# Third attention's keys computed during the expert tiles, and parts of the product-key and normalization work moved to GpSimd, in a new hand-written order

## The chip, the cores and the metric

One core of one Trainium2 chip runs the whole program in a single launch. The metric is the device time of that core in microseconds (us), as the median of several executions; lower is better. The engines are TensorE (PE: matmuls and transposes; its weight loads are listed apart as PEld), VectorE (DVE), ScalarE (ACT), GpSimd (POOL, which also issues some DMAs) and SyncE (SP, which here only issues DMAs).

## The reference

The input x is 2048 rows of 256 numbers. Eight sublayers follow each other, each of the form x = x + f(layernorm(x)). Besides x, the attentions read a context ctx of 16 x 128 rows of 128 numbers.

```
x = x + attention 1        (32 heads of 8, axial rotation of q and k)
x = x + product-key FFN    (4 heads: top 8 of 128 twice, top 8 of the 64 sums, 2048 experts)
x = x + attention 2        (16 query heads, 8 key/value heads of 128)
x = x + router, top 2 of 7 experts of width 256, and one shared expert
x = x + attention 3        (16 heads of 16, q and k layer-normalised per head)
x = x + ternary FFN        (width 682)
x = x + attention 4        (16 heads of 128, q and k RMS-normalised)
x = x + MXFP8 FFN          (width 1024)
```

The third attention treats the last 16 of each 128 context rows apart, with weights of their own:

```
y_dca, y_main = y[:, -16:], y[:, :-16]
k_dca, v_dca = split(y_dca @ Wkv_dca + bkv_dca);  k_dca = ln(k_dca, kn_dca_w, kn_dca_b)
q = ln(x @ Wq + bq, qn_w, qn_b)
k = ln(y_main @ Wk + bk, kn_w, kn_b);  v = y_main @ Wv + bv
out = (attn(q, k, v) + attn(q, k_dca, v_dca)) @ Wo + bo
```

`ln` works on each head's 16 numbers. Note that k and v of this attention depend on ctx and on weights alone, and not on x.

In the product-key FFN each row finds, for each of 4 heads, 8 pairs of keys. The kernel turns them into weights of experts by masks that are compared and multiplied, so that PE can do the gather as matmuls.

## The kernel before, in words

x stays in on-chip memory as 16 blocks of 128 rows. The work is cut into sublayers `s` (0 attention 1, 1 product-key FFN, 2 attention 2, 3 router, 8 expert tiles, 9 shared expert, 4 attention 3, 5 ternary FFN, 6 attention 4, 7 MXFP8 FFN), each of these into named steps per block `b` and part `c`, and `STEPS` says for each step on which engines it has instructions. Blocks of neighbouring sublayers run interleaved: a block needs only itself from the sublayer before, except where a table `ROOM` asks that an earlier sublayer is finished, because both use the same on-chip memory.

What sets the order is a text written by hand for each engine: in `ORDER` one letter stands for one step, and the n-th occurrence of a letter is the n-th part of that step. The engines run their queues in this order and wait for each other by counted semaphores (`wait_ge`). `BANKS` says which of the eight PSUM banks a step's result takes; `room` makes PE wait until the engine named in `TAKEN` has emptied the bank's previous content.

The steps that the change and the prediction touch, with the lines of the kernel before:

- Attention 3 (`small_heads` with s = 4): `qk` multiplies the block by Wq (L955, L956) and the context block by Wk (L960), and adds the last 16 context rows by Wkv_dca (L961), into one bank of 512 columns; `na` (DVE adds the bias, L1843; ACT squares), `nb` (DVE sums the squares per head, L1849; POOL adds epsilon and takes the power -1/2 of 128 x 32 numbers, L2526), `nc` (DVE multiplies, L1855), `tqk` (PE transposes q in four and k in four pieces, L990; ACT scales them into qT and kT), `vp` (values, L973, and those of the last 16 rows, L974), `mx` (score matmuls L1008, of which DVE takes the row maxima, and the same line again for the scores proper in `st`), and `tb`, `oT`, `out` for the result. POOL copies the last 16 context rows of every block into a tile of its own (L2503).
- Product-key FFN (`peer`): `ix` picks the indices of the 8 best pairs (DVE: compare L1946, multiply L1950, reduce L1952, each twice on 256 columns), `ae` makes a one-hot mask of 512 columns, `am` multiplies it by three parts of the weight (L2001, three times on 512 columns, four times per block), and `g` is the matmul on it.
- `lnA` and `lnB` normalise a block: statistics on DVE, the power on POOL, and the subtraction and multiplication on DVE (L1759).
- Router: `tab` (with a cast at L2133) makes the table of where rows go, `sc` scatters them by POOL's DMA into 38 tiles in DRAM (L2582), SP loads each tile (six tiles are in flight), the tiles run `tT`, `up`, `ga`, `dn` (L1200 to L1225), and POOL stores each (L2598). `cw` centres the third attention's weights on DVE, `init` fills its tiles on POOL (L2471 to L2492).

The step that reads a tile's matrices waits for the tile's load; POOL's store waits for ACT's result.

Of the kernel before, what the change touches and what calls it, by code (L numbers as in the profile page):

```python
# [28 lines left out]
RP, RQ, RV = 4, 3, 2  # L29

# [29 lines left out]
}  # L60
# [19 lines left out]
        "qwoppnooppwqplowompnlowpmoorpqnplopmonpoorlpooqmpnlooompxponpqppoolopxqprpomppnoooqlpopmoonolppmqppooolppxonqpopmoop"  # L80
        "pnxqppoxoppowrqppooosppxotosspqpttsssptpsttqtxsstusuxtuurvvvvsstutsrusvvtsytzuussttvvuttCusssutvvyuzvvrtussrututCsvv"
        "AuuAvvtBssytzuuBsvvsttvuurvssCuuttvrsvytvuttuzvsstsAsCuuvvyuvvBtsrttzsssAuutBvvuytzsuvvytCtuusszttyvuvvCussztuAvtruv"
        "vuAssCsyuzvvBttrtssAtutBsCusyvrtzuuBvvvsAsttystutCuzvvAuuBvvtBsssCtrtuutssCvyutzuvAvvtBussutytzuuCvvvrvAssAtytzuussB"
        "uttBvvAuBvvAuuCvyIBvzJuuCvvIIAJBKCJIIKyKzJJIIKKCJJADBKKEEFEEFFGGEFFHHEGEFFHEGGEFHHEGGEFFHEHFGEGFEHHEGGFFHHEGGEFFEHHF"
        "GEGFHEFGFHHEGGEFHHEFGGEFHHEGEGFFHHFEGGFEHHFEGGFHHEGEFEGFHHEFGGEFHHEGGFHEHEGGFFHHEGGFHHFGGHHIIJJIIIKKJJIIKKLJMJLKIIML"
        "JJLMJKKKNOPNKMPQONRSSSSTTPQONLRMUPSVQSSSTORTQLSNUSMSSRLTTOMUPSSVLLNVQPSSMTROTSSNSSQPOMTURTQLSSVNSSRTLTOPUNVSPUSQSSMO"
        "MRLTTQVSSMTSSRUTLLONVMPZZUSSSSNTOQPMLTLRVNSSZZQSSPNOTMTURQVSSPSSNTZORTMUSSSSPOQTWTWRQUSSVNSSRTONPSWXTSSSPOQXVQRTTUXW"
        "SSXWYWXWXSSRTWXXYYUXXVSSSSTTUYWXWXVTXXYVXUXYWXVXUYVXXWYYWXXXYWXXXXWYYXXX61W60Y60XXY6YY6262616120-1--1321312032234112"
        "34551410532314251322431455231403541253-241-52433524114-5530372121424123355438145531723124245432850124755432348811952"
        "+3453145510298137238142523134+1452455398871+4312432254559113+08435212487317504221455933+1130221435288421133245454355"  # L90
        "0988374+113422542591543+53288274215103432415915132831+84035231124245745523435198811732+41345504232159784+53318241228"
        "54859247373+4553898348784+45545598879+88+9+9+"),
    "V": (
        "ayahy((byabaabcabacbbacbaabdaeeceedeeceebaeeeeeeceedeebbeeffeecegedaeebefe(feeceedgeeeefceefebedeegaaeeffceeaeedbbgb"
# [2626 lines left out]
```

## Time and profile before

| what | value |
| --- | --- |
| median of 3 timed runs | 1972.67 us |
| lowest and highest of them | 1969.64 and 1978.3 us |
| the profiled execution | 1967.78 us, of this its span 1966.0 us |
| granted clock of TensorE, mean | 0.994 |
| PE busy | 1886.6 us (96%) |
| DVE busy | 1641.7 us (84%) |
| ACT busy | 1259.4 us (64%) |
| POOL busy | 791.2 us (40%) |

The span runs from the first to the last instruction. PE is busy for nearly all of it, so the share of the other engines says little by itself; what counts is in which stretch PE stands and for whom. A granted clock of 1.00 is PE's upper level of 2.4 GHz; 0.5 would be the lower of 1.2 GHz. The stages follow each other roughly so: attention 1 to 210 us, product keys to 550, attention 2 with the router to 938, tiles to 1070, attention 3 to 1270, ternary FFN to 1350, attention 4 and the MXFP8 FFN to the end.

### The profile page before, as it was taken

What the parts mean: (1) busy time and instruction counts of PE and PEld (TensorE: products, weight loads), DVE (VectorE), ACT (ScalarE), POOL (GpSimd) and SP (SyncE); (2) the same over time, 40 slices, a digit from 0 to 9 for tenths busy, and PEclk for the clock granted to TensorE, in tenths of its full rate; (3) what the DMA queues carried; (4) which work ended last, traced back from release to release, by engine and by line L of the source; (5) the groups of instructions that cost most, each with busy time, mean ns of one, the idle gap of its engine ahead of it and who ended that gap; (6) DMA issues with size and microseconds to landing.
All of it is one profiled execution on the core that took longest, in us unless ns stands there. A gap on an engine that the chain in (4) does not pass through costs nothing. (4 is left out here: it accounts for less than half of the span.)

```text
span 1966.0 us, 44931 instructions
## 1 busy us (share of the span) xinstructions
PE 1886.6 (96%) x15558; PEld 1502.2 (76%) x15558; DVE 1641.7 (84%) x4453; ACT 1259.4 (64%) x3210; POOL 791.2 (40%) x1160
## 2 busy tenths in 40 slices
PE   5999999999999999999799899999999999999999
PEld 3777899999988888888698777897565666566656
DVE  6888999999879987886755689886888998988897
ACT  3878988788865445554465566865676655656652
POOL 6443020000011223222213987513877666666640
PEclk9999999999999999999899999999999999999999
DMA  9500300000034434434222011016776455555540
GB/s 327 185 2 3 110 27 2 2 2 2 2 120 128 150 119 134 157 118 133 80 85 68 28 28 55 2 62 209 245 227 218 151 168 159 185 174 169 183 145 28
DMA packets 223642, 215.82 MB, mean 110 GB/s; under 512 B 25934, under 2 KB 198120, under 8 KB 222392
## 3 DMA queue, kind: packets, MB, share of 16 engines
q1 hardware_dynamic: 197176, 129.29, 21.7%
q0 software_dynamic: 26240, 83.65, 11.9%
q8 instruction: 125, 2.05, 0.4%
q14 instruction: 101, 0.83, 0.1%
HBM read 115.85 MB, written 96.99 MB: 108 GB/s over the span
## 5 line engine op out<-in xcount | busy, mean ns | idle before, releaser
L2462 POOL TENSOR_SCALAR sm<-sm 128x1 f32<-128x1 f32 x128 | 34.7, 271 | 503.8 <-DVE sm L1749 502.9
L1516 ACT ACTIVATE areaB<-i128h,workB 128x128 f16<-128x128 f16 x512 | 156.4, 393 | 0.5
L1677 ACT ACTIVATE workA<-pb,workA 128x128 f32<-128x128 f32 x256 | 113.8, 458 | 28.6 <-DVE workA L2343 26.5
L1090 PE MATMUL pb<-areaB 128*128 128x128 f32 x1024 | 123.2, 277 | 0.5 <-ACT workB L1506 0.5
L1134 PEld LDWEIGHTS pb<-xT,areaA 128*128 128x128 f32 x1024 | 119.1, 192 | 5.8 <-issue 5.1
L1134 PE MATMUL pb<-xT,areaA 128*128 128x128 f32 x1024 | 121.0, 275 | 0.0
L1090 PEld LDWEIGHTS pb<-areaB 128*128 128x128 f32 x1024 | 117.8, 192 | 2.0 <-ACT workB L1506 0.9
L1324 PE MATMUL pb<-areaA,workA 128*128 128x256 f32 x512 | 118.9, 380 | 0.1
L1468 ACT ACTIVATE areaA<-pb 128x512 f32<-128x512 f32 x192 | 105.2, 604 | 21.6 <-PE pb L1008 20.8
L2534 POOL DMA_DIRECT2D turn<-workA x64 | 36.9, 577 | 202.4 <-DVE workA L2046 194.2
L1157 PE MATMUL pb<-areaA,workA 128*128 128x256 f32 x512 | 117.2, 380 | 0.0
L1324 PEld LDWEIGHTS pb<-areaA,workA 128*128 128x128 f32 x512 | 96.0, 190 | 26.9 <-issue 14.8
L1106 PE MATMUL pb<-areaB,workB 128*128 128x256 f32 x512 | 113.9, 380 | 0.3 <-DVE workB L2010 0.3
L1543 ACT ACTIVATE workA<-workA 128x128 f32<-128x128 f32 x256 | 99.4, 392 | 19.1 <-DVE workA L2033 19.1
L1157 PEld LDWEIGHTS pb<-areaA,workA 128*128 128x128 f32 x512 | 95.3, 190 | 15.3 <-issue 3.5
L1106 PEld LDWEIGHTS pb<-areaB,workB 128*128 128x128 f32 x512 | 96.1, 190 | 13.5 <-DVE workB L2010 0.7
L1870 DVE TENSOR_REDUCE workA<-pb 128x4 f16<-128x512 f32 x128 | 83.0, 690 | 15.8 <-PE pb L1008 15.3
L2526 POOL TENSOR_TENSOR areaA<-areaA,neghalf 128x32 f32<-128x32 f32 x16 | 87.4, 5463 | 1.3
L1008 PE MATMUL pb<-workA 32*128 32x128 f16 (+2 forms) x2048 | 78.5, 251 | 8.4 <-DVE workA L1873 3.2
L2464 POOL TENSOR_TENSOR sm<-sm,neghalf 128x1 f32<-128x1 f32 x128 | 81.5, 637 | 10.7
L1310 PEld LDWEIGHTS pb<-workA 128*128 128x128 f32 x512 | 65.1, 191 | 26.7 <-issue 18.0
L1008 PEld LDWEIGHTS pb<-workA 32*128 32x128 f16 (+2 forms) x2048 | 57.5, 140 | 33.6 <-issue 28.5
(425 smaller groups left out, 5638.7 us busy)
## 6 DMA issues: line engine op xcount, KB each, us to landing
turn<-workA POOLq DMA_DIRECT2D x64, 256.0 KB, 2.5
workA<-turn SPq DMA_DIRECT2D x256, 64.0 KB, 2.1
turn3q<-workA POOLq DMA_DIRECT2D x64, 256.0 KB, 2.9
turn3k<-areaA POOLq DMA_DIRECT2D x64, 256.0 KB, 2.8
workB<-turn3q SPq DMA_DIRECT2D x256, 64.0 KB, 2.3
workA<-turn3k SPq DMA_DIRECT2D x256, 64.0 KB, 2.1
turn3p<-areaA POOLq DMA_DIRECT2D x64, 256.0 KB, 2.7
rows_in<-areaB SPq DMA_DIRECT2D x7, 2048.0 KB, 16.1
```

The costliest lines, as they stand in the source:

```text
L1008: m = eng.matmul(p[k][:, j * 128:(j + 1) * 128], one, two, start=True, stop=True)
L1090: m = eng.matmul(p[:, e * 128:(e + 1) * 128], w.ed[:, k, (4 * c + e) * 128:(4 * c + e + 1) * 128], xT[:, k, :], start=(k == 0), stop=(k == 1))
L1106: m = eng.matmul(p[:, 0:256], G[:, e, :], w.eu[:, e, :], start=(e == 0), stop=(e == 15))
L1134: m = eng.matmul(p[:, h * 128:(h + 1) * 128], w.wq[:, 4 * c + h, k], xT[:, k, :], start=(k == 0), stop=(k == 1))
L1157: m = eng.matmul(p[:, 0:256], u.OT[i][:, h], w.wo[:, 4 * c + h], start=(c == 0 and h == 0), stop=(c == 3 and h == 3))
L1324: m = eng.matmul(p[:, 0:256], u.OT[i][:, h], w.wo[:, 4 * c + h], start=(c == 0 and h == 0), stop=(c == 3 and h == 3))
L1468: eng.activation(u.P[n % RP], bank(s, tag, b, at)[:, :], ACT.Exp, scale=1.0 / math.sqrt(hd)).then_inc(freed(s, tag, b, at)[0], 1)
L1516: m = eng.activation(u.far[:, g], i128h[:, :], ACT.Square, bias=u.at[b % 2][:, 8 * c + g:8 * c + g + 1])
L1543: m = eng.activation(u.P[i][:, h], u.P[i][:, h], ACT.Exp, accum_out=u.den[i][:, h:h + 1], bias=u.nm[i][:, h:h + 1])
L1677: m = eng.activation(u.P[i][:, h], p[:, h * 128:(h + 1) * 128], ACT.Exp, accum_out=u.den[i][:, h:h + 1], bias=u.nb[i][:, h:h + 1], scale=u ...
L1870: eng.tensor_reduce(o[:, :, 24:25], p, AX.X, ALU.max, negate=True).then_inc(freed(s, tag, b, at)[0], 1)
L2526: eng.tensor_tensor(va, va, neghalf[:, 0:32], ALU.pow).then_inc(S["l2_rs"], 1)
```

## The change

It has three parts and a new order text for all engines.

1. **Keys early.** A new sublayer 10 of 18 blocks (`KEYS = NB + 2`) computes the third attention's keys while the expert tiles run. Its blocks 0 and 1 hold the last 16 context rows of eight context blocks each, so that one matmul of 512 columns gives keys and values of all of them; blocks 2 to 17 are the keys of the 16 context blocks. Each goes through bias, square, sum, power (now 128 x 16), multiplication, four transposes and scaling, and is written to DRAM (`keys4`, and `vals4` for the values). The third attention reads its keys and the 16 value rows back by SP (steps `kl`, `vl`). Its own `qk`, `na`, `nb`, `nc` handle q alone, on 256 columns, `vp` is one matmul and one copy, and the matmul on the difference of weights and POOL's copies are gone. The shared expert's `dn` uses bank 6 alone, and the keys use bank 7 for both steps.
2. **Product keys.** One compare of 512 columns instead of two of 256, the multiplication on POOL, one reduction; the third of the three masks of `am` is multiplied on POOL; the one-hot tile has two buffers.
3. **Normalization.** The subtraction and multiplication of `lnB` in attention 1 and in the product-key FFN move from DVE to POOL (`centred`).

```diff
-    1: (("lnA", 1, "VG"), ("lnB", 1, "V"), ("xT", 1, "TA"), ("q", 1, "TA"), ("sim", 1, "TA"), ("g", 4, "TA"),
-        ("tk", 1, "V"), ("tx", 1, "V"), ("pk", 1, "V"), ("ix", 1, "V"), ("tr", 1, "V"), ("bh", 4, "A"), ("ae", 4, "V"),
-        ("am", 4, "VT"), ("gm", 4, "V"), ("out", 1, "TV")),
+    1: (("lnA", 1, "VG"), ("lnB", 1, "G"), ("xT", 1, "TA"), ("q", 1, "TA"), ("sim", 1, "TA"), ("g", 4, "TA"),
+        ("tk", 1, "V"), ("tx", 1, "V"), ("pk", 1, "V"), ("ix", 1, "VG"), ("tr", 1, "V"), ("bh", 4, "A"), ("ae", 4, "V"),
+        ("am", 4, "VGT"), ("gm", 4, "V"), ("out", 1, "TV")),
...
+    10: (("k", 1, "T"), ("ka", 1, "AV"), ("kv", 1, "VG"), ("kc", 1, "V"), ("kt", 1, "TA"), ("ks", 1, "S")),
...
-        "eeabaababaacadbdcdbadfdZagdbdgehhhghdcigdfhhhhdgbigdhjhhhgdkcigafdhhehhgdbigdahhhjhdkcgfadghihhdbhdgihgehhdgchjgdfkh"
+        "Zaababbaacedbdcdbedaaafdgdbdghhahgdhecigdfhhhhdgbigdhjhhhgdkcgifdhhhhagdbigdahhhjhdkcgidfahhgdbhhgdeigdhehgcjhhghfdh"
...
-    (9, "dn"): lambda b, c: (("dn", 6 + b % 2),),
+    (9, "dn"): lambda b, c: (("dn", 6),),
...
+    (10, "k"): lambda b, c: (("k", 7),),
+    (10, "kt"): lambda b, c: (("kt", 7),),
...
+            def early_keys(step, b):
+
+                if step == "k":
...
+                    if b < 2:
+                        t.wait_ge(S["l2_init"], 1)
+                        m = eng.matmul(p[:, :], u10.last[b], w4.wd, start=True, stop=True)
+                    else:
+                        m = eng.matmul(p[:, 0:256], ctxT[:, (b - 2) * 128:(b - 1) * 128], w4.wk, start=True, stop=True)
+                    m.then_inc(full(10, "k", b)[0], 1)
+                else:
+                    t.wait_ge(S["l2_y"], b + 1)
+                    kp4 = u4.qp[b] if b < 2 else u10.kp[b % 2]
+                    p = room(10, "kt", b)
+                    for j in range(4):
+                        m = eng.transpose(p[:, j * 128:(j + 1) * 128], kp4[:, j * 128:(j + 1) * 128], ident)
...
+            def early_keys(step, b):
+                va = u10.va[b % 2]
+                g.wait_ge(S["l2_var"], b + 1)
+                eng.tensor_scalar(va, va, 1.0 / 16, 1e-6, ALU.mult, ALU.add).then_inc(*g.mark())
+                g.settle()
+                eng.tensor_tensor(va, va, neghalf[:, 0:16], ALU.pow).then_inc(S["l2_rs"], 1)
+
+            def peer(step, b, c):
+                u = u1
+                if step == "ix":
+                    g.wait_ge(S["v_next"], b + 1)
+                    e4 = u.eq.rearrange("p (h k j) -> p h k j", h=8, k=8)
+                    eng.tensor_tensor(e4, e4, bc(u.i8f.rearrange("p (h j) -> p h j", h=8), 2, [128, 8, 8, 8]),
+                                      ALU.mult).then_inc(S["g_pre"], 1)
+                elif step == "am":
...
+                    eng.tensor_tensor(u.Am[c % 2][:, 2], u.Ae[c % 2],
+                                      bc(ah[:, 3, 8 * c:8 * c + 8].rearrange("p (h g) -> p h g", g=2), 2, [128, 4, 64, 2]),
+                                      ALU.mult).then_inc(S["g_mul"], 1)
```

How the order text moves instructions is seen in the built programs, at three places.

POOL, between the router's last scatters (`rows_in`) and the stores of the tiles (`rows_out`); `workA` is on-chip memory that attention 3 will use. Before:

```order
L2462 TENSOR_SCALAR sm<-sm 128x1
L2464 TENSOR_TENSOR sm<-sm,neghalf 128x1
L2582 DMA rows_in<-areaA,workB 15104x256 x4
L2471 MEMSET workA 128x1024 x2
L2474 MEMSET workA 128x128 x3
L2476 MEMSET workA 128x1024 x2
L2490 TENSOR_SCALAR workA<-cst 128x16 x2
L2492 TENSOR_SCALAR workA<-cst 128x16 x2
L2490 TENSOR_SCALAR workA<-cst 128x16 x2
L2492 TENSOR_SCALAR workA<-cst 128x16 x2
L2598 DMA rows_out<-areaA 128x256 x38
```

After:

```order
L2594 MEMSET workA 128x1024 x2
L2609 COPY workA<-ctxT 128x128 x2
L2613 TENSOR_SCALAR workA<-cst 128x16 x4
L2615 MEMSET workA 128x16
L2616 MEMSET workA 128x16
L2615 MEMSET workA 128x16
L2616 MEMSET workA 128x16
L2724 DMA rows_in<-areaA,workB 15104x256 x6
L2740 DMA rows_out<-areaA 128x256
L2649 TENSOR_SCALAR areaA<-areaA 128x16
L2651 TENSOR_TENSOR areaA<-areaA,neghalf 128x16
L2740 DMA rows_out<-areaA 128x256 x6
```

The fills now stand ahead of the last three scatters, and the keys' powers stand between the stores of the tiles.

PE, in the tiles. Before (L1200 and L1201 transpose a tile, L1208, L1217 and L1224 to L1225 are its three matmul layers):

```order
L1208 MATMUL pb<-areaA 128x128 x8
L1224 MATMUL pb<-areaA 128x256
L1225 MATMUL pb<-areaA 128x256
L1224 MATMUL pb<-areaA 128x256
L1225 MATMUL pb<-areaA 128x256
L1200 MATMUL pb<-cst,areaA 128x128
L1201 MATMUL pb<-cst,areaA 128x128
L1217 MATMUL pb<-areaA 128x128 x4
```

After (L1116 is a key's matmul, L1123 its four transposes):

```order
L1116 MATMUL pb<-areaA,ctxT 128x256
L1281 MATMUL pb<-areaA 128x128 x4
L1272 MATMUL pb<-areaA 128x128 x4
L1264 MATMUL pb<-cst,areaA 128x128
L1265 MATMUL pb<-cst,areaA 128x128
L1288 MATMUL pb<-areaA 128x256
L1289 MATMUL pb<-areaA 128x256
L1288 MATMUL pb<-areaA 128x256
L1289 MATMUL pb<-areaA 128x256
L1123 MATMUL pb<-cst,workA 128x128 x4
```

Between a key's matmul and the next transposes PE now has one tile's matmuls or somewhat more.

DVE, in the product-key FFN, where the indices of a block are picked. Before:

```order
L1940 CAST workB<-workB 128x64
L2001 TENSOR_TENSOR areaB<-workB 128x512 x3
L1946 TENSOR_TENSOR workB<-cst,workB 128x256
L1950 TENSOR_TENSOR workB<-workB 128x256
L1952 TENSOR_REDUCE workB<-workB 128x32
L1946 TENSOR_TENSOR workB<-cst,workB 128x256
L1950 TENSOR_TENSOR workB<-workB 128x256
L1952 TENSOR_REDUCE workB<-workB 128x32
L1954 SCALAR_TENSOR_TENSOR workB<-workB 128x32
```

After:

```order
L2048 TENSOR_SCALAR workB<-workB 128x32
L2050 CAST workB<-workB 128x64
L2052 TENSOR_TENSOR workB<-cst,workB 128x512
L2056 TENSOR_REDUCE workB<-workB 128x64
L2058 SCALAR_TENSOR_TENSOR workB<-workB 128x32
```

Two compares, two multiplications and two reductions have become one compare and one reduction, with POOL's multiplication between them.

## Rows read from the trace of the kernel before

**Rows 1.** The page's line of busy time, share of the span and instructions.

```profile
PE 1886.6 (96%) x15558; PEld 1502.2 (76%) x15558; DVE 1641.7 (84%) x4453; ACT 1259.4 (64%) x3210; POOL 791.2 (40%) x1160
```

**Rows 2.** Windows: length, then busy PE, PEld, DVE, ACT, POOL, clock, DMA share, GB/s.

```profile
50.00:210.00 160.00, 156.61 (x2630) 116.81 (x2632) 135.61 (x337) 129.87 (x241) 59.07 (x114) 1.00 0.17 57
210.00:550.00 340.00, 335.23 (x3673) 314.00 (x3664) 310.37 (x1332) 297.03 (x728) 24.83 (x48) 1.00 0.06 21
...
938.00:948.00 10.00, 0.50 (x3) 0.09 (x1) 9.48 (x22) 1.24 (x2) 5.98 (x14) 0.77 0.04 14
948.00:1070.00 122.00, 120.05 (x893) 112.89 (x894) 66.06 (x142) 71.57 (x200) 23.67 (x41) 0.98 0.26 83
1070.00:1270.00 200.00, 187.16 (x2175) 156.78 (x2173) 160.37 (x459) 128.52 (x268) 158.59 (x140) 0.98 0.11 33
```

**Rows 3.** Timeline of PE in attention 3: start, duration, line [idle before <-releaser].

```profile
1118.96 1.09 PE L990 MATMUL pb<-cst,workA 128*128 128x128 f32 x8 [0.36 <-DVE workA L1855]
1119.88 0.27 PE L934 MATMUL pb<-cst,xn 128*128 128x128 f32 x1
...
1121.70 1.17 PE L1008 MATMUL pb<-workA 18*128 18x128 f32 x32 [1.44 <-DVE workA L1873]
...
1123.77 0.59 PE L960 MATMUL pb<-areaA,ctxT 128*128 128x256 f32 x2
1124.20 0.59 PE L961 MATMUL pb<-areaA,workA 128*128 128x256 f32 x2
1124.63 0.27 PE L1052 MATMUL pb<-cst,areaA 128*128 128x128 f32 x1
```

**Rows 4.** Groups of DVE in attention 3, 1070 to 1270 us.

```profile
L1855 DVE TENSOR_TENSOR workA<-workA,areaA 128x512 f32<-128x512 f32 x16 | 11.8, 740 | 4.4 <-POOL areaA L2526 3.6 <-PE pb L1018 0.8
...
L1849 DVE TENSOR_REDUCE areaA<-areaA 128x32 f32<-128x512 f32 x16 | 10.8, 676 | 2.2 <-ACT areaA L1426 2.1
```

**Rows 5.** Groups of POOL: busy, mean ns of one, idle before.

```profile
L2526 POOL TENSOR_TENSOR areaA<-areaA,neghalf 128x32 f32<-128x32 f32 x16 | 87.4, 5463 | 1.3
...
L2568 POOL TENSOR_TENSOR workA<-workA,neghalf 128x4 f32<-128x4 f32 x64 | 71.3, 1113 | 5.3
```

**Rows 6.** Timeline of PE in attention 4, two matmuls of 512 columns.

```profile
1409.88 1.02 PE L1294 MATMUL pb<-areaA,xT 128*128 128x512 f32 x2
1410.74 1.02 PE L1295 MATMUL pb<-areaA,xT 128*128 128x512 f32 x2
```

**Rows 7.** Groups of DVE by shape in the product keys, 210 to 540 us.

```profile
L2001 DVE TENSOR_TENSOR areaB<-workB 128x512 bf16<-128x512 bf16 x93 | 33.8, 417 | 0.2
...
L1950 DVE TENSOR_TENSOR workB<-workB 128x256 f32<-128x256 f32 x30 | 12.7, 425 | 1.0
```

**Rows 8.** Windows of 4 us in attention 3, columns as in rows 2.

```profile
1107.00:1111.00 4.00, 2.11 (x40) 1.71 (x39) 3.09 (x10) 3.23 (x5) 3.83 (x3) 0.96 0.01 2
...
1199.00:1203.00 4.00, 2.61 (x39) 1.84 (x32) 2.87 (x12) 2.46 (x7) 4.00 (x1) 0.98 0.00 0
...
1111.00:1115.00 4.00, 3.51 (x35) 3.37 (x36) 0.00 (x0) 2.65 (x6) 3.51 (x3) 0.61 0.00 0
1203.00:1207.00 4.00, 4.00 (x16) 3.46 (x16) 3.97 (x6) 2.85 (x6) 2.28 (x3) 0.59 0.00 0
```

**Rows 9.** Attention 4: POOL's products (group, one), DVE's L1759 (one; group from 1450 us).

```profile
L2562 POOL TENSOR_TENSOR workA<-workA 128x512 f32<-128x512 f32 x64 | 67.3, 1053 | 35.9 <-DVE workA L2348 35.1
...
1502.88 1.03 POOL L2562 TENSOR_TENSOR workA<-workA 128x512 f32<-128x512 f32 x1
...
1502.99 1.06 DVE L1759 TENSOR_SCALAR areaB<-x,sm 128x256 f32<-128x256 f32 x1
...
L1759 DVE TENSOR_SCALAR areaB<-x,sm 128x256 f32<-128x256 f32 x14 | 7.1, 511 | 2.0 <-POOL sm L2464 2.0
```

**Rows 10.** Timeline of the gap ahead of the tiles, one DVE and one POOL row.

```profile
936.05 4.84 DVE L2133 CAST workB<-workB 128x8 uint32<-128x8 f32 x1
...
939.00 1.86 POOL L2476 MEMSET workA<- 128x1024 f32 x2
```

More of the change, by code:

```diff
@@ L80 @@
[L80 to L83, printed above, removed]
@@ L1451, in small_heads @@
                     src = bank(4, "v", b)[:, 0:256].rearrange("p (h e) -> p h e", e=16)
-                    for k in range(2):
-                        m = eng.activation(u.vt[b % RV][:, :, 17 * k:17 * k + 16], src, ACT.Copy, scale=side[k])
-                    m.then_inc(freed(4, "v", b)[0], 1)
+                    eng.activation(u.vt[b % RV][:, :, 0:16], src, ACT.Copy, scale=in_main).then_inc(freed(4, "v", b)[0], 1)
                 elif step == "vp":
@@ L1486, in small_heads @@
                         m.then_inc(freed(s, "oT", b)[0], 1)
+            def early_keys(step, b):
+                u = u10
+                if step == "ka":
+                    a.wait_ge(*freed(10, "k", b))
+                    if b >= 2:
+                        a.wait_ge(S["l2_var"], b - 1)
+                    eng.activation(u.sq[b % 2], u.y[b % 2].rearrange("p (h e) -> p h e", e=16),
+                                   ACT.Square).then_inc(S["l2_sq"], 1)
+                else:
+                    a.wait_ge(*loaded(4))
+                    a.wait_ge(*full(10, "kt", b))
+                    if b in (2, 3):
+                        a.wait_ge(S["k_d"], 160)
+                    elif b >= 4:
+                        a.wait_ge(S[f"hbm{b % 2}"], 16 * (b // 2))
+                    src, dst = bank(10, "kt", b)[:, :].rearrange("p (t n) -> p t n", n=128), u.kT[b % 2]
+                    if b < 2:
+                        m = eng.activation(dst, src, ACT.Identity, scale=w4.nwc[:, 2:3], bias=w4.nwc[:, 5:6])
+                    else:
+                        m = eng.activation(dst[:, :, 0:112], src[:, :, 0:112], ACT.Identity, scale=w4.nwc[:, 1:2], bias=w4.nwc[:, 4:5])
+                    m.then_inc(freed(10, "kt", b)[0], 1)
             def peer(step, b, c):
@@ L2472, in small_heads @@
                     if s == 4:
-                        for k in range(3):
-                            eng.memset(u.cd[k], 0.0)
+                        for k in range(2):
+                            eng.memset(u10.kp[k], 0.0)
                     for k in range(RV):
@@ L2487, in small_heads @@
                         ones = ones_sq[:, 0:16].unsqueeze(2)
+                        g.wait_ge(*ctx_here(0))
+                        g.wait_ge(*ctx_here(NB - 1))
+                        for k in range(2):
+                            eng.tensor_copy(u10.last[k].rearrange("p (b n) -> p b n", n=16),
+                                            ctxT[:, :].rearrange("p (b n) -> p b n", n=128)[:, 8 * k:8 * k + 8, 112:128])
                         for j in range(2):
@@ L2609, in gpsimd_program @@
                     normalize(s, b)
+                elif step == "lnB" and s == 1:
+                    centred(1, b)
                 elif s in (0, 4):
                     small_heads(s, step, b, c)
+                elif s == 10:
+                    early_keys(step, b)
                 elif step == "ws":
@@ L2617, in gpsimd_program @@
                     tiles(step, b, c)
+                elif s == 1:
+                    peer(step, b, c)
                 elif s == 2:
```

411 lines of the change are left out of this document (244 added, 167 removed), and 6 rows, old and new, of tables (STEPS, TAKEN).

## The prediction

> **What bounds the kernel now.** The line of busy time comes first [rows 1]: TensorE (PE) is busy 1886.6 of 1966.0 us, VectorE (DVE) 1641.7, GpSimd (POOL) 791.2. So a step is paid for where PE executes it, and everything else pays only through the 79 us in which PE stands. Next come the windows by stage [rows 2]: in each the reader compares PE's busy time with the length, and then looks at who else is nearly full. Attention 1 (50 to 210 us) leaves PE 3.4 us idle and the product keys (210 to 550) 4.8, with DVE at 310.37 of 340 there. Between router and expert tiles (938 to 948) nearly all of the 10 us is lost. The tiles (948 to 1070) run PE 120.05 of 122 while DVE, ACT and POOL have half or more of their time free. The third attention (1070 to 1270) has the largest loss that the change touches, 12.8 us, with POOL at 158.59 and DVE at 160.37 of 200. The timeline of PE in that stage [rows 3] names what it waits for there: the normalised heads (1.44 us before the score matmuls L1008, 0.36 us before the transposes L990, both released by DVE). The groups of DVE [rows 4] go one step back: of the 4.4 us that it stood before L1855, 3.6 ended with POOL's power L2526, which takes 5.46 us [rows 5].
>
> **Part 1, the matmuls.** Per block the third attention loses three 256-column calls (L960, L961, L974) and four of its eight L990 transposes. From start to start a call takes 0.43 us (1123.77, 1124.20, 1124.63) and the eight transposes 0.92 us (1118.96 to 1119.88) [rows 3], so 3 x 0.43 + 0.46 = 1.75 us leave per block, 28.0 us in 16. Into the tiles come 16 calls of 256 columns (6.9 us), two of 512 at 0.86 [rows 6] (1.7) and 18 x 4 transposes (18 x 0.46 = 8.3): 16.9 us. The tiles have no idle PE time to hide them in, so they are paid in full. Net: **-11.1 us**. This part is nearly certain, since it is the same work at the same price.
>
> **Part 2, what the third attention gets besides.** POOL's power goes from 128x32 to 128x16. No row shows 16 columns; 4 columns take 1.11 us and 32 take 5.46 [rows 5], which are the two ends. Between them 28 columns cost 4.35 us, 0.155 each, so I take 1.11 + 12 x 0.155 = 2.97 us. POOL then has 16 x 2.5 = 40 us less work in this stage and its link of the chain is 2.5 us shorter. Three DVE passes of 512 columns (0.74 and 0.68 us, the third put at 0.68 too, [rows 4]) become 256 wide, for which 0.42 is the row of a pass of that width [rows 7]: 16 x 0.84 = 13.4 us. But PE's work falls from 187.16 to 159.2 and the stage with it, to about 167 us, in which DVE still needs 160.37 - 13.4 = 147, 88% against 80% now. A shorter chain wins back idle time and a fuller DVE costs some: of 12.8 us I take **-5**, with 0 and -12 as ends. In addition two stretches of 4 us ran with a granted clock of 0.61 and 0.59 [rows 8], so mostly at the lower level of 1.2 GHz, and in the 4 us ahead of each PE had been busy for only 2.11 and 2.61 us, at a clock of 0.96 and 0.98. At 0.6 of the clock 4 us lose 1.6; if those waits go, **-3.2**; ends 0 and -3.2.
>
> **Part 3, the product keys and attention 1.** DVE gives away one of three expert masks four times per block (0.417 us each, 64 in all: 27 us) and the index product; two compares, two products and two reductions of 256 columns (the product's 0.425 taken for all six, 2.55 us) become one compare and one reduction of 512, 0.68 each by L1849: 1.19 x 16 = 19 us [rows 4, 7]. The row normalisation (L1759; I take 0.41, the length of a pass of 256 columns [rows 7], though its mean in the last stage is 0.511 [rows 9]) goes to POOL in both stages, 6.5 us each. That is 52 us of 310 in stage 1. PE is idle there for only 4.8 us in 340, and 3.4 in 160 in attention 1, so the relief can show only in these 8.2 us: I take **-3**, ends 0 and -8. The new double buffer of the one-hot removes a wait on the same engine and is in that sum.
>
> **Part 4, the gap ahead of the tiles.** A cast of eight columns on DVE took 4.84 us there, to 940.89, while POOL filled buffers until 940.86 [rows 10]; nothing in its size explains more than some tenths. In the new order the fills stand ahead of the last scatters, so this cast is freed: about -4.5. Against it, all weights of the third attention are centred before the router's last steps: passes of 256 columns at 0.42 over wq, wk, wd and three biases, some 16 passes or 7 us of DVE, which the router's chain may have to wait for, and the last three scatters are queued on POOL behind fills, copies and small constants (1.86 for the fills of 1024 columns, the rest put at twice that). I take **0**, ends -5 and +7.
>
> **Part 5, the keys in the tiles off PE.** Per key: DVE 3 x 0.42, ACT one square and one scaling (put at 1.1 together, twice the share of a DVE pass), POOL one power at 2.97 and a small pass ahead of it, put at 0.3. For 18 keys that is 23 us on DVE (66.06 of 122 busy), 20 on ACT (71.57) and 59 on POOL (23.67) [rows 2], in a stage that grows to about 139 us. All fit, so the work costs nothing as long as no one waits in order; that condition is the rival E. DMAs: ten small writes, 16 key writes and 32 reads on SP's queue, on which the tile loads stand six tiles ahead of their use (6 x 3.2 = 19 us), and the DMA engines are busy for 0.26 of the stage. Cost 0.
>
> **Sum.** -11.1 - 5 - 3.2 - 3 + 0 = -22.3. The profiled execution took 1967.78 us (span 1966.0), so 1945.5. The median of the three timed runs, 1972.67, lies 4.9 us higher, so I forecast **1950**.
>
> **What the skill says against it.** A POOL pass over SBUF can hold DVE up: L1759 on DVE ran 1.06 us beside a 1.03 us product of POOL on 512 columns [rows 9], which is 0.65 us more than 0.41, the price that I put on this pass. The group shows how seldom: 14 of these passes in the last stage average 0.511 [rows 9], 0.1 us more each. The Trainium skill's page GPSIMD Engine Reference, section 1 (Specifications), says that GpSimd shares its SBUF interfaces with VectorE and contends with instructions in a two-port mode or with two SBUF inputs, and its section 4.1 advises VectorE for elementwise products, as GpSimd is about 2x slower. The trace agrees on speed: 1.05 us for 512 columns on POOL against 0.68 on DVE (L1849) [rows 4, 9]. Read strictly, the rule makes this change a loss in the product keys, which is rival D.
>
> **The rivals.**
> - **A, the forecast** (gain of 12 to 32 us, 1941 to 1961). For it: PE full everywhere but in the places named. Chance 0.50.
> - **B, only the matmuls count**: -11.1 and the third attention now bound by DVE (147 of 167). 1972.7 - 11 = 1962. Against it: the wait of 3.6 us on the power. 0.18.
> - **C, more idle is won**: all of the 12.8 and 8.2 us, the clock and 5 of the gap: -11.1 - 12.8 - 3.2 - 8.2 - 5 = -40, 1932, or lower where the new order also closes idle time outside the touched stages. 0.10.
> - **D, POOL's products hold DVE in the product keys.** Five products per block, 80 in all, 1.05 us each. If each held a DVE pass as L1759 was held (1.06 - 0.41 = 0.65 us), DVE would lose 52 us, all that it was relieved of; with its queue in order the masks also come later by 1.05 - 0.42 us. PE would gain nothing there and lose some 10 us to waits: 1972.7 - 11.1 - 5 - 3.2 + 10 = 1963, and 1973 with 20. Against it: the mean of 0.511, and the power of 5.46 us with POOL busy for 79% of the third attention, in which DVE's L1849 keeps 0.68. 0.12.
> - **E, slower: the keys stall the tiles.** Bank 7 serves both a key's matmul and its transposes, and a key runs through DVE, ACT, DVE, POOL (3 us) and DVE, about 6 us, before PE may transpose; a tile passes each 122/38 = 3.2 us, and PE's new order has some one to three tiles of work between the two. POOL issues the power in one queue with the stores of the tiles, which wait for ACT, so a power may come a tile late. If each of 18 keys costs one tile's time: 58 us, about 2008. The forecast is lost at (1962.8 - 1950)/18 = 0.7 us per key, and the kernel is measurably slower from (1982.6 - 1950)/18 = 1.8 us per key. 0.10.
>
> **How the numbers follow.** 0.5%, 9.9 us, is about what a measurement of this kernel can tell from no change: faster means below 1962.8, slower above 1982.6. All of A and C and half of B are faster (0.50 + 0.10 + 0.09), with a little of D: 0.70. Same: half of B, most of D, the mild part of E: 0.19. Slower: 0.11. The range leaves out the strong cases of E and the far part of C: 1922 to 1972. The likeliest case's own range is 1941 to 1961.
>
> **What would show it.** Tile stage: about 17 us longer and PE still full; if PE waits for bank 7 or for L1123's input there, E. Third attention: about 33 us shorter, power near 3 us, no stretch at half clock; if it is 28 shorter with PE waiting for DVE, B. Product keys: PE's idle time down from 4.8; if DVE's busy time stays near 310 in spite of the 52 us removed, with casts and scalar passes at over 1 us, D. The gap of 10 us: the 4.84 us cast gone and PE's first tile no later than before; if the centring passes stand between the router's last steps, part 4 was wrong. The forecast as a whole is wrong if the sum of the gains outside the matmuls is under 0 or over 25 us.

## The result, and the profile after

| kernel | median, us | ratio to before, 95% interval |
| --- | --- | --- |
| before, beside the change | 1972.67 | |
| with the change | 1990.51 (1987.38 to 1997.62, 5 runs) | 1.0094 (1.0076 to 1.0111) |

The change made the kernel 18 us slower. The forecast was 1950 with a range of 1922 to 1972, so it was wrong in sign. The profiled execution of the changed kernel has a span of 1987.2 us, 21.2 more than the profiled one before (1966.0), which was itself a quick one of its kernel, 4.9 us under the median; so a sum over stages gives 21.2 and the medians 17.8.

First the page's line of busy time of the changed kernel, the answer to [rows 1].

```profile
PE 1886.9 (95%) x15506; PEld 1498.7 (75%) x15506; DVE 1647.6 (83%) x4353; ACT 1249.4 (63%) x3196; POOL 938.0 (47%) x1293
```

POOL has 147 us more, as planned. But DVE, which gave work away, is as busy as before, and PE is as busy although the trace has 52 matmul records less (15506 against 15558). Stage by stage the loss is found with the first and last start of the last matmul of each stage. The rows below are of the lines that end the product keys, attention 2, the tiles, the ternary FFN, attention 4 and the last FFN; first the changed kernel, then before (line, duration min/median/max in ns, first to last start in us, forms).

```profile
L1170 PE MATMUL pb<-areaB,workB x512: 379/379/500, 236.9 to 587.3; 128*128 128x256 f32 x171
...
L1221 PE MATMUL pb<-areaA,workA x512: 379/379/463, 598.3 to 933.7; 128*128 128x256 f32 x171
...
L1289 PE MATMUL pb<-areaA x76: 379/379/379, 976.2 to 1095.8; 128*128 128x256 f32 x76
...
L1340 PE MATMUL pb<-areaB,workB x192: 272/273/283, 1280.6 to 1358.1; 128*128 128x256 f16 x192
...
L1388 PE MATMUL pb<-areaA,workA x512: 379/379/483, 1402.6 to 1950.3; 128*128 128x256 f32 x171
...
L1427 PE MATMUL pb<-areaB,workB x256: 379/379/634, 1553.9 to 1984.2; 128*128 128x256 f32 x128
```

```profile
L1106 PE MATMUL pb<-areaB,workB x512: 379/379/483, 237.5 to 567.0; 128*128 128x256 f32 x171
...
L1157 PE MATMUL pb<-areaA,workA x512: 379/379/463, 583.2 to 917.8; 128*128 128x256 f32 x171
...
L1225 PE MATMUL pb<-areaA x76: 379/379/379, 959.5 to 1063.2; 128*128 128x256 f32 x76
...
L1276 PE MATMUL pb<-areaB,workB x192: 272/273/273, 1276.6 to 1354.1; 128*128 128x256 f16 x192
...
L1324 PE MATMUL pb<-areaA,workA x512: 379/379/483, 1394.4 to 1928.9; 128*128 128x256 f32 x171
...
L1363 PE MATMUL pb<-areaB,workB x256: 379/379/454, 1543.7 to 1963.0; 128*128 128x256 f32 x128
```

Read as differences, the changed kernel is 0.6 us ahead at the first result of the product keys and 20.3 behind at the last; 15.9 behind at the end of attention 2; 16.7 behind at the first tile's end, 32.6 at the last tile's; 4.0 behind at the end of the ternary FFN; 21.4 at the end of attention 4 and 21.2 at the end. So there are four large movements: **product keys +20.9, tiles +15.9, third attention (with the ternary FFN behind it) -28.6, and attention 4 with the last FFN +17.2**, in which not one instruction was changed. Two are small: attention 2 gave 4.4 back, and the gap ahead of the tiles cost 0.8.

In the product keys the groups of DVE, 210 to 560 us of the changed kernel, answer to [rows 7]:

```profile
L2107 DVE TENSOR_TENSOR areaB<-workB 128x512 bf16<-128x512 bf16 x60 | 40.1, 707 | 1.4 <-PE pb L1163 1.2
...
L2107 DVE TENSOR_TENSOR workB<-workB 128x512 bf16<-128x512 bf16 x62 | 38.2, 656 | 0.5 <-PE pb L1163 0.3
L2028 DVE FIND_INDEX8 workB<-workB 128x8 uint32<-128x128 f32 x120 | 31.6, 283 | 0.0
...
L2056 DVE TENSOR_REDUCE workB<-workB 128x64 f32<-128x512 f32 x15 | 10.1, 674 | 7.8 <-POOL workB L2658 7.8
```

A mask product takes 0.707 and 0.656 us in the mean where the same instruction took 0.417; the two that are left cost DVE about what the three cost before. The index searches (L2028) keep their 0.283 us. But these means are of two sorts of instruction, as the next rows show: all 128 mask products (duration min/median/max in ns), and one meeting with POOL's product (start, duration).

```profile
L2107 DVE TENSOR_TENSOR workB<-workB x64: 392/417/1489, 213.8 to 565.5; 128x512 bf16<-128x512 bf16 x64
L2107 DVE TENSOR_TENSOR areaB<-workB x64: 406/418/1498, 220.2 to 572.2; 128x512 bf16<-128x512 bf16 x64
...
492.22 1.16 POOL L2666 TENSOR_TENSOR workB<-workB 128x512 bf16<-128x512 bf16 x1 [2.15 <-DVE workB L2098]
492.40 1.59 DVE L2107 TENSOR_TENSOR workB<-workB 128x512 bf16<-128x512 bf16 x2
```

The median is still 0.417. Counted one by one in the trace, 39 of the 128 took over 0.8 us, most of them 1.26, and 37 of these 39 overlapped POOL's mask product. In the meeting shown POOL's product starts 0.18 us ahead and ends at 493.38; the first of the two on DVE takes 1.26 us and ends 0.28 us after it, and the second takes 0.41. So a mask product is either not held at all or held until POOL's is over.

The groups of POOL in the same stretch:

```profile
L2666 POOL TENSOR_TENSOR workB<-workB 128x512 bf16<-128x512 bf16 x31 | 35.6, 1150 | 88.6 <-DVE workB L2098 70.8 <-PE pb L1163 17.8
L2666 POOL TENSOR_TENSOR areaB<-workB 128x512 bf16<-128x512 bf16 x30 | 34.7, 1158 | 47.4 <-PE pb L1163 23.9 <-DVE workB L2098 23.5
L2658 POOL TENSOR_TENSOR workB<-workB 128x512 f32<-128x512 f32 x15 | 19.7, 1311 | 71.7 <-DVE workB L2052 71.7
L2581 POOL TENSOR_SCALAR areaA<-x,sm 128x256 f32<-128x256 f32 x12 | 17.5, 1458 | 0.3
```

And the clock of PE, in windows of 4 us (columns as in [rows 2]): PE's waits in this stage are followed by stretches at the lower clock, which the stage did not have before. The longest of these waits, 3.9 us up to 486.8 us, was for POOL's normalisation (L2581), which stood in POOL's queue behind the index product and two mask products.

```profile
320.00:324.00 4.00, 2.98 (x51) 2.99 (x52) 3.08 (x7) 2.38 (x6) 1.34 (x3) 0.69 0.00 0
356.00:360.00 4.00, 3.95 (x41) 3.98 (x42) 3.47 (x20) 0.00 (x0) 2.06 (x3) 0.62 0.02 4
484.00:488.00 4.00, 1.10 (x14) 1.04 (x15) 4.00 (x8) 1.46 (x6) 3.61 (x4) 0.67 0.00 0
488.00:492.00 4.00, 4.00 (x57) 3.77 (x54) 3.83 (x13) 1.15 (x1) 1.06 (x1) 0.50 0.01 4
```

The two together are the stage's loss: from 215 to 575 us PE was busy for 344.1 of 360 us against 357.6 before, which is 13.5 us more idle, and three windows of 40 us had a granted clock of 0.96, 0.96 and 0.91 instead of 1.00, which is worth another 6.8.

### The profile page after: what moved, and what is told of

Read it like the earlier page. It is cut to its first block, busy times and chain, and to the rows that moved or that the text cites. A ratio compares the mean times of both kernels' runs of the same rounds, so it can differ in the third digit from the quotient of the medians.

```text
span 1987.2 us, 45165 instructions
## 1 busy us (share of the span) xinstructions
PE 1886.9 (95%) x15506; PEld 1498.7 (75%) x15506; DVE 1647.6 (83%) x4353; ACT 1249.4 (63%) x3196; POOL 938.0 (47%) x1293
## 4 chain that ended last, share of the span: by engine, by line
PE 41%; DVE 13%; issue 7%; DMA 7%; POOL 5%; SPq 3%; ACT 2%; DVEq 0%; POOLq 0%; ACTq 0%
PE pb L1221 5%; PE pb L1198 4%; SPq L885 2%; PE pb L1213 2%; PE pb L1206 2%; PE pb L1170 2%; PE pb L1272 2%; PE pb L1047 2%; PE pb L1281 2%; PE pb L1427 1%; PE pb L1153 1%; PE pb L1076 1%; PE pb L1332 1%; DMA turn3p<-areaA 1%; PE pb L1388 1%
## 5 line engine op out<-in xcount | busy, mean ns | idle before, releaser
L1601 ACT ACTIVATE workB<-areaB,cst 128x1024 bf16<-128x1024 f16 x64 | 73.5, 1148 | 14.3 <-PE pb L1163 12.4
L2572 POOL TENSOR_TENSOR sm<-sm,neghalf 128x1 f32<-128x1 f32 x128 | 76.9, 601 | 10.7
```

Source lines behind the costliest of these rows:

```text
L2572: eng.tensor_tensor(rs, rs, neghalf[:, 0:1], ALU.pow).then_inc(S[f"ln_rs{odd}"], 1)
```

## The experiments

All ran beside the kernel before. Two theories stood at the start: H, that POOL's products hold DVE's while they run; O, that the new order is worse in attention 4 and the last FFN. Each had its rival, named in the expectations.

**e1, the third mask back on DVE.** The changed kernel, with this edit and the waits for POOL's mask removed:

```diff
-        ("am", 4, "VGT"), ("gm", 4, "V"), ("out", 1, "TV")),
+        ("am", 4, "VT"), ("gm", 4, "V"), ("out", 1, "TV")),
...
-                    for k in range(2):
+                    for k in range(3):
                         m = eng.tensor_tensor(u.Am[c % 2][:, k], u.Ae[c % 2],
```

> The changed kernel with one thing undone: the third of the three expert masks is multiplied on DVE again, 64 products of 128x512 less on POOL; order, keys and the rest as changed. Theory H (POOL's products hold DVE's mask products up, 0.66 to 0.71 us each in the changed kernel against 0.417 before): DVE's two products fall back to about 0.42 and the product-key stage wins back most of its 17 us, so 1974 to 1982 us. Rival R (DVE was delayed by the index product and the normalisations on POOL, or by the new order in this stage): no gain, 1988 us or more, since DVE also has 27 us more to do.

Measured: 1974.3 us, ratio to before 1.0022 (1.0007 to 1.0038). So 16.2 us of the loss (14 by the two ratios) hang on the 64 mask products of POOL. DVE makes 64 products more than in the changed kernel, 27 us at 0.417, and yet the stage, which had grown by 20.9 us, has grown by 4.5 only.

**e2, the whole front as before.** All product-key work and both normalisations on DVE, and the order text of before for all parts that run before about the middle of attention 2.

> The changed kernel with the first part undone: masks, index product and row normalisations all on DVE, and the order of before on all engines until about the middle of attention 2; the early keys and the rest of the new order stay. Whatever the cause inside the product keys, the 20 us that the start and the product keys lost should come back: 1968 to 1973 us. If it stays above 1980, the loss is carried by something else than the product keys.

Measured: 1974.63 us, 1.0009 (0.9993 to 1.0025). It gains no more than e1 and landed 1.6 us above the expected window. In its trace the product keys are back (0.7 us above before), so the 20 us did return in that stage; attention 2, which had given 4.4 us back in the new order, gives 1.1 here, and the profiled execution is 3 us late at the first product-key result already, as that of e4 is with the same order there: executions differ by that much.

**e3 and e4, the tail of the order text.** The parts from about 1300 us on are put in the other kernel's order: e3 is the changed kernel with the tail of before, e4 the kernel before with the tail of the change. No other line differs. The first of the lines for PE, in e3:

```diff
-        "WTWRUQSSVNSSRTTNOSPWXSSSPWQOXVQRTTUXVXWYWXWXUSSSSRWTXXYYVXXWSSSSTXTXUYYTWXXVXUXUYWXVYVXWXXYXXYWYWXXWXXWYXXXX16YY6XX6"
+        "WTWRUQSSVNSSRTTNOSPWXSSSPWQOXVQRTTUXVXWYWXWXUSSSSRWTXXYYVXXWSSSSTXTXUYYTWXXVXUXUYWXVYXVXXWYYWXXXYWXXXXWYYXXX61W60Y60"
```

> The changed kernel with the order of before on all engines from the end of the third attention on (attention 4 and the last FFN, whose instructions are the same in both kernels). Theory O (the new order of this part costs 17 us, since nothing else of it was changed): 1971 to 1976 us. Rival N (the order there does not matter, the 17 us come from the state in which the part is entered, weights or blocks arriving late): 1987 to 1992 us.

> The kernel before, with the new order from the end of the third attention on, and nothing else changed. Theory O: 17 us slower than before, 1986 to 1992 us. Rival N: 1970 to 1975 us, no change.

Measured: e3 1977.57 us, 1.0037 (1.0019 to 1.0055), 12.9 less than the changed kernel and 1.6 above the window. e4 1988.42 us, 1.0081 (1.0055 to 1.0107), 16 more than before. Rival N is out: the same instructions cost 16 us more in the new order alone (12.9 by e3). In the traces the part behind the ternary FFN takes 608.9 us before and 608.6 in e3, 626.1 in the changed kernel and 625.8 in e4. The waits of PE in e4 in this part, 1361 to 1989 us (what waited for whom, total us, times, longest):

```profile
PE pb L1321 <- DMA areaA<-turn3p: 4.9, 8, 1.4
PE pb L1315 <- ACT workB L1710: 4.2, 3, 3.3
PE pb L1343 <- ACT areaB L1694: 3.7, 2, 3.4
PE pb L1315 <- ACT workA L1667: 2.3, 4, 1.2
```

In the kernel before the like list, 1355 to 1966 us, is:

```profile
PE pb L1310 <- ACT workA L1662: 3.1, 3, 2.0
PE pb L1338 <- DMA areaB<-qw: 1.9, 1, 1.9
PE pb L1363 <- ACT workB L1705: 1.5, 2, 0.8
PE pb L1316 <- DMA areaA<-turn3p: 1.5, 2, 1.0
```

The score matmuls (L1315, before L1310), which wait 3.1 us for ACT's copies in this list of before, wait 6.5 in the rows of e4, once for 3.3 us behind another block's work on ACT (L1710), and the probabilities that are turned by DMA come late eight times in place of three (there is a second such row before, of 1.1 us). By windows over the whole part, PE stands 31.0 of 629 us in e4 against 20.2 of 612 before; the rest of the loss is in its busy time, 598.0 against 591.8, with a mean clock of 0.99 against 1.00.

**e5, the early keys alone.** The edits of e2 and e3 together: what is left of the change is the new stage and the new order between the middle of attention 2 and the end of the third attention.

> Only the early keys of the change are left: masks, index product and row normalisations on DVE; the order of before up to the middle of attention 2 and again from the end of the third attention on, the new order between them. By the traces so far the stages between the experts and the end of the third attention won 13 us net (tiles 16 longer, third attention 28.6 shorter, gap 2 longer), and nothing else should be left of the change. If the three parts simply add: 1958 to 1963 us. Rival: the gain in the middle is given back in the last part, as a transfer or a clock drop there: 1968 to 1974 us.

Measured: 1962.03 us, 0.9943 (0.9925 to 0.9962). The three parts add up, and this one is faster than before by 10 us.

**e6, e1 and the tail of e3.**

> The changed kernel with the third mask on DVE again and the order of before from the end of the third attention on; the index product and both normalisations stay on POOL. If the two losses add (16.2 us for the masks, 12.9 for the order): 1959 to 1964 us. If they overlap (both runs removed the same loss): 1970 to 1976 us.

Measured: 1965.64 us, 0.9965 (0.995 to 0.998), 1.6 above the window: 24.9 of the 29.1 us that the two won singly. The losses are different ones; the 4 us that are missing from the sum are no more than the intervals leave open.

**e7, all three masks on DVE, and POOL's product beside them for nobody.** No matmul but the last waits for POOL's result. One wait of DVE for POOL stays: its one-hot still waits until POOL has read the buffer two products back; e10 keeps that wait too.

```diff
                     if two:
                         g.wait_ge(*full(1, "m", *two))
-                    eng.tensor_tensor(u.Am[c % 2][:, 2], u.Ae[c % 2],
+                    if two:
+                        g.wait_ge(S["g_mul"], nth(*two, 4))
+                    eng.tensor_tensor(u1.spare[c % 2], u.Ae[c % 2],
```

> DVE makes all three masks, as in e1, and POOL multiplies the third one too, at the same place as in the changed kernel, into memory that nobody reads; no matmul waits for it. Theory H (POOL's product holds DVE's products up while it runs): DVE's mask products take 0.6 to 0.7 us again though nobody needs POOL's result, and the run is slower than e1 by 10 us or more, 1984 to 2000 us. Rival W (PE or DVE waited for POOL's slower result, not for the memory): as e1, 1972 to 1977 us.

Measured: 2005.45 us, 1.0167 (1.0139 to 1.0195), 31 us above e1 and outside the window on the slow side. Rival W is out. The groups of DVE's mask products and of POOL's product, 215 to 560 us, in e7:

```profile
L2114 DVE TENSOR_TENSOR areaB<-workB 128x512 bf16<-128x512 bf16 x87 | 48.7, 612 | 0.6 <-PE pb L1170 0.4
L2114 DVE TENSOR_TENSOR workB<-workB 128x512 bf16<-128x512 bf16 x84 | 42.6, 559 | 0.2
...
L2675 POOL TENSOR_TENSOR areaA<-workB 128x512 bf16<-128x512 bf16 x57 | 67.8, 1194 | 132.0 <-DVE workB L2105 109.8 <-PE pb L1170 11.5 <-issue 9.9
```

and in e1, where POOL only has the index product and the normalisations:

```profile
L2108 DVE TENSOR_TENSOR areaB<-workB 128x512 bf16<-128x512 bf16 x96 | 38.5, 455 | 1.2 <-PE pb L1166 1.0
L2108 DVE TENSOR_TENSOR workB<-workB 128x512 bf16<-128x512 bf16 x93 | 35.0, 430 | 1.1 <-PE pb L1166 0.7 <-issue 0.2
```

In e7 38 of 192 mask products took over 0.8 us, as good as the 39 of 128 in the changed kernel, so the mean is lower with three than with two; in e1 there were 5.

**e8, index product and the second normalisation on DVE too**, in the new order.

> The changed kernel with masks, index product and the product-key stage's row normalisation all on DVE (the first normalisation stays on POOL), in the new order. Against e1 it tells what the index product and that normalisation on POOL are worth. DVE gets 1.1 us per block more and is freed from POOL's 1.3 us product and 1.46 us normalisation. If these two also cost by holding DVE: 1968 to 1972 us. If their relief is worth something: 1976 to 1982 us. If neither: as e1, 1972 to 1976 us.

Measured: 1970.89 us, 0.9995 (0.998 to 1.001), 3.4 less than e1. So these two seem to cost a little as well, though they take 1.1 us per block off DVE; the two intervals just meet, so this is at the edge of what they tell. There the mask products are back at 0.417 and 0.418 us.

**e10, a power beside the masks.** As e7, but POOL takes a power of 128x4 numbers where it multiplied.

```diff
-                    eng.tensor_tensor(u1.spare[c % 2], u.Ae[c % 2],
-                                      bc(ah[:, 3, 8 * c:8 * c + 8].rearrange("p (h g) -> p h g", g=2), 2, [128, 4, 64, 2]),
-                                      ALU.mult).then_inc(S["g_mul"], 1)
+                    eng.tensor_tensor(area[0][:, 11264 + 4 * (c % 2):11268 + 4 * (c % 2)], cst[:, C_ONE:C_ONE + 4], neghalf[:, 0:4],
+                                      ALU.pow).then_inc(S["g_mul"], 1)
```

> As e7, but where POOL multiplied the mask a second time it now takes a power of 128x4 numbers (1.11 us by the rows, against 1.15 for the product), into memory that nobody reads. If DVE is held by the product's traffic to on-chip memory: no slowdown against e1, 1972 to 1978 us, and DVE's mask products at 0.42 us. If it is POOL's occupancy (its queue, what stands behind the product on it, the semaphores): as e7, 2000 us or more.

Measured: 1973.68 us, 1.0011 (0.9999 to 1.0023), as e1. Its rows, of DVE and of POOL:

```profile
L2113 DVE TENSOR_TENSOR areaB<-workB 128x512 bf16<-128x512 bf16 x96 | 37.5, 445 | 1.4 <-PE pb L1169 1.3
L2113 DVE TENSOR_TENSOR workB<-workB 128x512 bf16<-128x512 bf16 x93 | 35.8, 439 | 0.8 <-PE pb L1169 0.6
...
L2674 POOL TENSOR_TENSOR areaA<-cst,neghalf 128x4 f32<-128x4 f32 x63 | 71.8, 1145 | 130.5 <-DVE workB L2104 97.6 <-issue 20.7 <-PE pb L1169 12.2
```

These groups of POOL take 72 us here against 68 with the product in e7, at the same places and with the same semaphores, and hold nobody up: 48 mask products overlapped the power and nothing else of POOL's, and the longest of them took 0.425 us. So the 31 us of e7 come from something that the product does and the power does not, and neither from POOL being occupied nor from DVE's wait for it. That this is the product's traffic to on-chip memory is likely, as it reads and writes 512 columns and the power 4, but a product of few columns was not run.

The traces show that it all happens in this one stage. From the first to the last start of its last matmul:

| kernel | product keys, us | against before |
| --- | --- | --- |
| before | 329.5 | |
| changed | 350.4 | +20.9 |
| e1, third mask on DVE | 334.0 | +4.5 |
| e7, the same, POOL's product for nobody | 366.4 | +36.9 |
| e10, the same, a power for nobody | 334.2 | +4.7 |
| e8, index product and normalisation on DVE too | 332.9 | +3.4 |
| e2, and the order of before | 330.2 | +0.7 |

**e11, the new tail from about 1690 us only**, in the kernel before.

> The kernel before with the new order only from about 1690 us on, in place of 1300 us in e4. If the new order loses at many places (6 us before 1410, 9 between 1650 and 1810, the rest at the end): about half of e4's 16 us, 1979 to 1983 us. If it is one place early in attention 4 that sets everything later: 1972 us, no change. If it is all late: 1988 us.

Measured: 1983.86 us, 1.0052 (1.0034 to 1.007), 0.9 us above the window for many places. So 11 of the 16 us arise after 1690 us and some 5 before it: it is not one place that sets everything later.

**e12, a second power ahead of each of the third attention's**, in e5.

```diff
+                    eng.tensor_tensor(spare, cst[:, C_ONE:C_ONE + 16], neghalf[:, 0:16], ALU.pow).then_inc(*g.mark())
                     eng.tensor_scalar(va, va, 1.0 / 16, 1e-6, ALU.mult, ALU.add).then_inc(*g.mark())
```

> e5 with a second power of 128x16 on POOL ahead of each of the 16 in the third attention, result unused: the link of the chain is 3 us longer, about as long as before the change. If the shorter power is what the change won in that stage beside the matmuls (as the forecast had it, 5 us and the clock): 1966 to 1971 us. If the power is hidden behind other work: as e5, 1960 to 1964 us.

Measured: 2003.75 us, 1.0166 (1.0148 to 1.0183): 41.7 us more than e5, 2.6 us for each of 16 blocks, far outside both windows. In the traces 35 us of it, 2.2 per block, arise between the end of the tiles and that of the ternary FFN: PE stands 19 us longer there (31.7 of 301 us against 12.7 of 267), and the rest is lost at a granted clock of 0.91 against 0.97. The waits in it, 1080 to 1330 us, of PE and of DVE:

```profile
PE pb L1031 <- DVE workA L1941: 9.4, 7, 3.4
```

```profile
DVE workA L1941 <- POOL areaA L2647: 29.1, 14, 3.9
```

**e9, the best version**: e8 with the tail of e3.

> The version that the runs so far point to: early keys, all product-key work on DVE (masks, index product, that stage's normalisation), the new order up to the end of the third attention, the order of before from there on. It is e8 with the tail of e3. If the parts add: 1970.9 - 12.9 = 1958 us, and better than e5. If the front of the new order is worth nothing: 1962 us as e5. If it loses again: over 1966.

Measured: 1959.4 us, 0.9942 (0.9925 to 0.9959), 13.3 us faster than before and 31 faster than the changed kernel. It cannot be told from e5 by its ratio, so the front of the new order (with the first normalisation, which stays on POOL here) is worth nothing that these runs show.

## Why the prediction was wrong, point by point

- **Part 1, the matmuls: right.** The tiles grew by 15.9 us (16.9 forecast, of which 1.7, the two calls of 512 columns, ran just ahead of the mark) and the third attention lost 28.6 (28.0 forecast for the work alone). Net 12.7 against 11.1, and the kernel with nothing else (e5) is 10.4 us faster in the median.
- **Part 2, what the third attention gets besides: wrong.** The power of 16 columns took 3.04 us, 2.97 forecast. But of "-5" and "-3.2" nothing came: the 28.6 us that the stage lost are its matmuls. PE stood 11.9 of 246 us in it, against 12.9 of 276 before (1064 to 1340 us), and a stretch at half clock is there again behind a wait. The rows are two windows of the changed kernel:

```profile
1097.00:1343.00 246.00, 234.08 (x3055) 201.66 (x3055) 202.54 (x608) 156.93 (x335) 128.36 (x149) 0.99 0.25 76
...
1136.00:1140.00 4.00, 4.00 (x38) 3.44 (x35) 1.37 (x4) 2.65 (x5) 3.92 (x4) 0.50 0.11 33
```

  The step that failed is the reading of the idle time as the price of a chain that is too long. Here are PE's largest waits in the stage, before (1070 to 1340 us) and after (1100 to 1345):

```profile
PE pb L1008 <- DVE workA L1873: 3.2, 3, 1.6
PE pb L990 <- DVE workA L1855: 1.8, 3, 0.9
...
PE pb L1047 <- DVE workA L1954: 1.9, 2, 1.1
PE pb L1026 <- ACT workA L1504: 1.6, 4, 0.7
PE pb L1076 <- ACT areaA L1526: 1.2, 2, 1.1
```

  The 1.44 us ahead of the score matmuls [rows 3] were not a wait for the normalised heads, as the prediction has it: L1873 is DVE's reduction for the row maxima, which empties their bank. Only the wait of the transposes for L1855, 1.8 us in the stage, hung on the power. That wait is gone, and DVE waits 1.0 us for the power (L2644 there) instead of 3.6. PE's listed waits for DVE fell from 6.4 to 3.0 us, but those for ACT rose from 5.0 to 8.4. So the number was rival B's (only the matmuls count), but its reason was not: DVE was busy for 202.5 of 246 us, and most of PE's waits ended with ACT. e12 shows that the chain has little slack in the new order: 3 us more on the power cost 2.2 us per block in the stage. Before, a power of 5.46 us was carried with 3.6 us of waiting in the whole stage [rows 4], so it may be the order, written around a given length of the chain, that decides whether a link is hidden. That last step is argued, not shown: the old order was not tried with a shorter power.
- **Part 3, the product keys: the step that failed first.** "I take -3, ends 0 and -8" put the hold of DVE by POOL's products at nothing; the stage grew by 20.9 us. Rival D had the right mechanism and nearly its price (52 us of DVE; found 33 us on the 128 mask products, more on the one-hots beside them, 0.491 against 0.417, and 7.8 us of waits for the index product). It gave 1963 us, or 1973 with 20 us of waits, and a chance of 0.12. What was mis-sized:
  - The mean of 0.511 [rows 9] hid two sorts of pass. After 1350 us six passes of L1759 in the kernel before met POOL's product L2562; two took 0.38 us and four took 0.80, 1.06, 1.37 and 1.54. The row that shows the longest:

```profile
L1759 DVE TENSOR_SCALAR xn<-x,sm x64: 371/404/1539, 9.5 to 1809.2; 128x256 f32<-128x256 f32 x64
```

  - In the last stage the two kinds of work meet by chance. In the product keys POOL's product and DVE's first one wait for the same one-hot, so they meet often: 55 of the 128 mask products overlapped POOL's, and 37 of them were held. A hit costs up to 0.84 us (1.26 against 0.42) and not 0.65 us.
  - The other argument against D, L1849 at 0.68 beside POOL's power, said nothing of products: a power does not hold DVE (e10), and a reduction of this kind is not held by the product either (L2056 took 0.67 and 0.69 us in the two cases where it met one).
  - POOL's normalisation took 1.458 us, more than 1.05 for 512 columns in the nearest row, and PE waited 3.9 us for it once.

  The -3 for DVE's relief did not come: e8 leaves most of it out and is no slower than e1.
- **GpSimd beside VectorE.** Products of the two hold each other up (mask products of 0.612 and 0.559 us in e7 against 0.455 and 0.430 in e1), and a power does not (0.445 and 0.439 in e10). The Trainium skill's page GPSIMD Engine Reference, section 1 (Specifications), says that GpSimd shares its SBUF interfaces with VectorE and contends with instructions that have two SBUF inputs. For the product the trace agrees, for the power it does not. Section 4.1 of the page advises VectorE for elementwise products; e1 agrees, 16.2 us faster with them there. The factor of about 2 that the prediction took from it was checked there against a reduction (0.68 us); the mask product itself takes 1.15 us on GpSimd and 0.417 on VectorE.
- **Part 4, the gap: the number right, as a balance of two terms.** 0.8 us against 0. The cast took 0.17 us instead of 4.84, and PE's wait for the tiles' rows fell from 9.8 to 3.7 us. Against it, centring passes of 0.42 us (L1854 to L1858) did stand between the router's last steps, which the prediction had named as a sign that this part was wrong, and PE waited 5.7 us for DVE there against 1.1 before. The ends of -5 and +7 had both in them; that they cancel so well is luck.
- **Part 5, the keys off PE: right.** POOL's power took 2.98 us in the tiles and no tile waited for a key; rival E, which I gave for the slower side, did not occur.
- **The order text was not priced: the second step that failed.** The prediction costed steps and left 616 us after the ternary FFN out, as nothing is changed in them; only rival C speaks of the order outside the touched stages, and as a gain. There the new order cost 16 us (e4; 12.9 by e3, 17.2 in the profiled executions). The sum had no term for it.

The profiled executions give the whole account. Forecast and found: product keys -3 and +20.9, attention 2 nothing and -4.4, gap 0 and +0.8, tiles +16.9 and +15.9, third attention -36.2 and -28.6, the part behind the ternary FFN 0 and +17.2, and -0.6 ahead of the product keys. That is -22.3 forecast and +21.2 found. What gave attention 2 its 4.4 us was not tried apart; the kernels with the front of the old order (e2, e5) have 1 to 2 of them.

Open stays which engine's text makes the tail slow. It was not tried apart, since an order on one engine without the others can stop the program.

## What to carry to other kernels

Before an elementwise product is moved to GpSimd, look at what VectorE does in the same microsecond: if both start from the same semaphore, a hold that is rare elsewhere becomes common (here 39 of 128 products), and the work that VectorE keeps gets slower by as much as the work it gave away. Do not price such a hold from the mean of a group: look for its longest instruction, too. Price a hand-written order as a change of its own wherever its text differs, also in stages whose instructions are the same; swapping the tails of two orders tells its cost in two runs. And lengthening a link does not tell what shortening it is worth: 3 us more on the power cost 41.7 us (e12), and 2.4 us less, in a new order, had won nothing.

## What the runs showed of the hardware

- A GpSimd product of 128x512 bf16 takes 1.04 us at the least and 1.15 in the mean. Beside it a VectorE product of the same kind is either not held or held until it is over: 39 of 128 took over 0.8 us, most of them 1.26, where the 44 that met nothing of GpSimd's took 0.40 to 0.42. VectorE's index search (0.283 us) and a reduction of 128x512 f32 (0.67 us, two cases) keep their times beside it.
- A GpSimd power of about the same length (1.145 us, 128x4) does not hold VectorE's products: 48 that overlapped it alone took at most 0.425 us (e10).
- GpSimd's subtract-and-scale of 128x256 f32 took 1.46 us, longer than its product of 128x512 bf16 (1.15), though it has half the columns. Seven mask products that overlapped it alone took 0.41 to 0.42 us.
- The power's price is linear in the columns: 1.11 us for 4, 2.98 and 3.04 for 16, 5.46 for 32.
